# Routed stage of a fused two-layer kernel: the down product one slot later, both transpositions side by side, three homes for expert weights

## The reference

```python
def _moe_forward(hidden_states, gate_w, w_gate, w_up, w_down, sw_gate, sw_up, sw_down):
    x = hidden_states.reshape(-1, d)                  # 2048 x 512
    scores = jax.nn.softmax(x @ gate_w, axis=-1)
    topk_w, topk_idx = jax.lax.top_k(scores, K)       # K = 2 of E = 8
    comb = comb.at[jnp.arange(T)[:, None], topk_idx].add(topk_w)
    g = jax.nn.silu(jnp.einsum('td,edh->teh', x, w_gate)) * jnp.einsum('td,edh->teh', x, w_up)
    routed = jnp.einsum('teh,ehd,te->td', g, w_down, comb)   # h = 352
    shared = jax.nn.silu(x @ sw_gate) * (x @ sw_up) @ sw_down
    return (routed + shared).reshape(b, s, d)
```

## Time and profile before

| | us |
|---|---|
| median of the runs, and their range | 1068.06 (1067.4 to 1068.07) |
| the profiled execution | 1068.25 |
| its span, from the first to the last record | 1066.5 |
| TensorE busy in it | 1018.3 |
| first gather of tile 2 to the end of TensorE's work (routed stage) | some 782 to 1050 |
| last record of POOL, which issues the last scatter_add | 1057.7 |

### The profile page before, as it was taken

One profiled execution on the slowest core, in us unless ns is written; L12 is line 12 of the kernel. 1 busy time (PEld: TensorE's weight loads), 2 busy tenths in 40 slices (PEclk: granted clock), 3 DMA queues, 4 the chain that ended last, 5 costly groups with the idle time before them and its releaser, 6 DMA issues.

```text
span 1066.5 us, 14883 instructions
## 1 busy us (share of the span) xinstructions
PE 1018.3 (95%) x4893; PEld 842.1 (79%) x4895; DVE 527.5 (49%) x884; ACT 315.0 (30%) x550; POOL 360.8 (34%) x353
## 2 busy tenths in 40 slices
PE   8889999999999999999989999999989999999993
PEld 5668887888888887888757777778878999999992
DVE  3688877455575555545666333574551324442100
ACT  3733332111121112111232020301044454455551
POOL 4213344510000000000243000022067988988873
PEclk9989999999999999999999999999999999999997
DMA  6676643544333434454336000003255565665443
GB/s 210 211 244 207 201 130 116 170 133 144 132 126 113 156 131 162 130 178 138 117 110 194 30 12 32 9 0 114 106 164 151 158 158 108 143 152 148 79 59 40
DMA packets 51322, 136.41 MB, mean 128 GB/s; under 512 B 8708, under 2 KB 10004, under 8 KB 50772
## 3 DMA queue, kind: packets, MB, share of 16 engines
q1 hardware_dynamic: 37268, 109.22, 30.2%
q0 software_dynamic: 12432, 25.71, 12.2%
q10 hardware_dynamic: 1584, 1.02, 0.3%
HBM read 96.85 MB, written 39.07 MB: 127 GB/s over the span
## 4 chain that ended last, share of the span: by engine, by line
PE 81%; POOL 6%; DMA 4%; DVE 3%; issue 2%; ACT 1%; SPq 1%; PEldq 0%; POOLq 0%; PEld 0%; DVEq 0%; ACTq 0%
PE ps_y L1657 6%; PE ps_y L1659 6%; PE ps_y L1658 6%; PE ps_h L1617 5%; PE ps_h L1616 5%; PE ps_h L1615 5%; PE ps_u L1670 3%; PE ps_u L1669 3%; DMA out_x<-yt,slot_tok 2%; PE ps_y L1826 2%; POOL xg_lo L759 2%; PE ps_y L1827 2%; PE ps_h L1810 2%; PE ps_h L1903 2%; PE ps_h L1811 2%
## 5 line engine op out<-in xcount | busy, mean ns | idle before, releaser
L1192 DVE TENSOR_TENSOR h<-h,wb 128x512 f32<-128x512 f32 x64 | 44.4, 694 | 170.7 <-ACT h L898 163.7
L892 ACT ACTIVATE h<-ps_h,bias 128x512 f32<-128x512 f32 x64 | 44.0, 689 | 235.1 <-PE ps_h L1624 235.1
L1657 PE MATMUL ps_y<-w_hi,g_hi 128*128 (+1 forms) x256 | 103.2, 403 | 10.2 <-DVE g_lo L1200 10.2
L1659 PE MATMUL ps_y<-w_hi,g_lo 128*128 (+1 forms) x256 | 102.4, 400 | 0.0
L1658 PE MATMUL ps_y<-w_lo,g_hi 128*128 (+1 forms) x256 | 102.2, 399 | 0.0
L1615 PE MATMUL ps_h<-xt_hi,w_hl 128*128 128x512 f32 x256 | 100.0, 391 | 0.7 <-ACT lg_t L841 0.7
L1617 PE MATMUL ps_h<-xt_hi,w_hl 128*128 128x512 f32 x256 | 100.4, 392 | 0.0
L1616 PE MATMUL ps_h<-xt_lo,w_hl 128*128 128x512 f32 x256 | 100.2, 391 | 0.0
L1450 DVE CAST eg_hi<-e_raw 128x704 fp32r<-128x704 f32 x32 | 17.1, 594 | 136.9 <-PE ps_y L1928 124.5
L898 ACT ACTIVATE h<-ps_h,bias 128x512 f32<-128x512 f32 x64 | 43.9, 688 | 116.0 <-PE ps_h L1637 116.0
L753 POOL DMA_INDIRECT out_x<-yt,slot_tok x39 | 62.8, 1611 | 24.0 <-issue 12.0
(11 more groups left out here) (318 smaller groups left out, 2521.1 us busy)
## 6 DMA issues: line engine op xcount, KB each, us to landing
w_hl<-w1s_d SPq DMA_DIRECT2D x49, 704.0 KB, 4.1
w1s_d<-w_hl SPq DMA_DIRECT2D x16, 704.0 KB, 5.9
e_raw<-in_wgu SPq DMA_DIRECT2D x8, 1408.0 KB, 7.3
w_raw<-in_w1b SPq DMA_DIRECT2D x16, 608.0 KB, 4.7
x_in<-in_x SPq DMA_DIRECT2D x4, 1024.0 KB, 6.4
xres<-in_x SPq DMA_DIRECT2D x16, 256.0 KB, 4.5
acc<-x_d SPq DMA_DIRECT2D x4, 1024.0 KB, 8.0
xc_d<-xc SPq DMA_DIRECT2D x4, 1024.0 KB, 5.0
```

The source lines that it names most:

```text
L892: nc.scalar.activation(h0[u][:], ps_h[:, u, :], ACT.Gelu_apprx_tanh, bias=bias1[:, f:f + 1])\
L1192: tt(h1[u][:], h1[u][:], wb[:, v, :], ALU.mult).then_inc(gch, 1)
L1657: mm(ps_y[:, j, :], g_hi[u][:, cols], sl(w2_hi), start=first, **kw)
L1659: mm(ps_y[:, j, :], g_lo[u][:, cols], sl(w2_hi), start=False, **kw)
```

## The change

- In slot t TensorE now runs gate(t+1), up(t+1), turn_x(t+2), turn_g(t), down(t-1). The down product comes one slot after its transposition. In the last slots down(36), down(37), turn_g(38) and down(38) follow each other.
- `rgt_hi` and `rgt_lo` exist twice. ACT runs silu(t+1), up copy, x_high(t+2), g_high(t), weigh(t-1). POOL runs x_low(t+2), products(t+1), g_low(t), gather(t+5), scatter_add(t-1).
- Expert weights have three homes, 0, 2 and 3, of one tensor `expert`; the small buffers lie in the place of home 1. Expert e waits for the last tile of expert e-3.
- The home of an expert is e mod 3 and no longer e mod 2, which can't be read from the packed number by a bit. So `count_tokens` makes a second packed table, `home_tab` (base 4), after `etab`; TensorE's program waits for both and reads both. `WINDOW` is 6 instead of 5, since a pass of four slots now needs the experts of six tiles. Five slots are written out ahead of the loop instead of four.

```diff
-    WINDOW = 5
+    WINDOW = 6
+    HOMES = (0, 2, 3)
...
             for t in range(SLOT_TILES):
-                g_low(t)
+                if t + 2 < SLOT_TILES:
+                    x_low(t + 2)
                 if t + 1 < SLOT_TILES:
                     products(t + 1)
-                if t + 2 < SLOT_TILES:
-                    x_low(t + 2)
+                g_low(t)
...
                 if nxt:
                     silu(t + 1, 1 - u)
-                g_high(t, first=stored is None and n == 0)
-                if nxt:
                     up(t + 1, 1 - u)
                 if nxt2:
                     x_high(t + 2)
-                weigh(t, n, stored)
+                if nxt:
+                    g_high(t, u, first=isinstance(t, int) and t == 0)
+                if not isinstance(t, int) or t:
+                    weigh(t - 1, (n - 1) % 4, stored)
...
                 nc.vector.tensor_copy(etab[:], etab_g[:]).then_inc(etab_ok, 1)
+
+                dve.wait_ge(etab_ok, 1)
+                for turn in (6.0, 3.0):
+                    link(nc.vector.tensor_scalar(etab_g[:], etab_f[:], turn, -3.0, ALU.is_ge, ALU.mult))
+                    link(tt(etab_f[:], etab_f[:], etab_g[:], ALU.add))
+                link(nc.vector.tensor_scalar(etab_g[:], etab_f[:], 1.0, None, ALU.is_ge))
+                link(tt(etab_f[:], etab_f[:], etab_g[:], ALU.add))
+                link(nc.vector.memset(etab_g[:], 0.0))
+                link(nc.vector.tensor_copy(etab_g[:, 0:windows], etab_f[:, WINDOW - 1:ETAB]))
+                for n in reversed(range(WINDOW - 1)):
+                    link(nc.vector.scalar_tensor_tensor(out=etab_g[:, 0:windows], in0=etab_g[:, 0:windows],
+                                                        scalar=4.0, in1=etab_f[:, n:n + windows],
+                                                        op0=ALU.mult, op1=ALU.add))
+                nc.vector.tensor_copy(home_tab[:], etab_g[:]).then_inc(etab_ok, 1)
...
-                if e >= 2:
-                    tiles = dve.value_load(last_tile[0:1, e:e + 1], min_val=0, max_val=SLOT_TILES)
+                if e >= 3:
+                    tiles = dve.value_load(last_tile[0:1, e - 1:e], min_val=0, max_val=SLOT_TILES)
...
-            pe.wait_ge(etab_ok, 1)
+            pe.wait_ge(etab_ok, 2)
...
-                packed = pe.value_load(etab[0:1, bass.ds(t, 1)], min_val=0, max_val=E ** WINDOW - 1)
-                return [(packed // E ** n % E, packed // E ** n % 2) for n in range(WINDOW)]
+                names = pe.value_load(etab[0:1, bass.ds(t, 1)], min_val=0, max_val=E ** WINDOW - 1)
+                places = pe.value_load(home_tab[0:1, bass.ds(t, 1)], min_val=0, max_val=4 ** WINDOW - 1)
+                return [(names // E ** n % E, places // 4 ** n % 4) for n in range(WINDOW)]
...
-            def slot_tile(t, u, x_buf, n, this, after, nxt=True, nxt2=True):
...
-                if nxt:
-                    gate_or_up(t + 1, 1 - u, after, 0)
-                turn_g(t)
-                if nxt:
-                    gate_or_up(t + 1, 1 - u, after, 1)
+            def slot_tile(t, u, x_buf, n, behind, after, nxt2=True):
...
+                gate_or_up(t + 1, 1 - u, after, 0)
+                gate_or_up(t + 1, 1 - u, after, 1)
                 if nxt2:
                     turn_x(t + 2, x_buf, n)
-                down_routed(t, u, this)
+                turn_g(t)
+                if behind is not None:
+                    down_routed(t - 1, 1 - u, behind)
```

More of the change, by code:

```diff
@@ L1895, in gate_or_up, with w @@
                 o = (ps_h, ps_y)[k][:, u, 0:H1]
[L1896 removed]
+                def w(low, c):
+                    at = low * GU + (2 * c + k) * H1
+                    return expert[:, bass.ds(b, 1), at:at + H1].rearrange("p a n -> p (a n)")
                 for c in range(DC):
[L1898 to L1899 removed]
+                    mm(o, xg_hi[:, c, :], w(0, c), start=(c == 0), stop=False)
+                    mm(o, xg_hi[:, c, :], w(1, c), start=False, stop=False)
                 if k == 0:
@@ L1902, in gate_or_up @@
                 for c in range(DC):
-                    last = mm(o, xg_lo[:, c, :], w(eg_hi, c), start=False, stop=(c == DC - 1))
+                    last = mm(o, xg_lo[:, c, :], w(0, c), start=False, stop=(c == DC - 1))
                 last.then_inc((rgate_done, rup_done)[k], 1)
@@ L1950, in _ @@
             pe.wait_ge(sy_read, NS * TPS)
-            ahead = WINDOW - 1
-            for t in range(ahead):
-                slot_tile(t, t % 2, (t + 2) % 4, ((t + 2) // 4 + 1) * 16, e[t], e[t + 1])
-            with pe.Fori(1, (SLOT_TILES - 2) // ahead) as m:
-                e = experts(m * ahead)
-                for u in range(ahead):
-                    slot_tile(m * ahead + u, u % 2, (u + 2) % 4, (m + (u + 2) // 4 + 1) * 16, e[u], e[u + 1])
-            rest = range((SLOT_TILES - 2) // ahead * ahead, SLOT_TILES)
-            e = experts(SLOT_TILES - WINDOW)[WINDOW - len(rest):] + [None]
-            for n, t in enumerate(rest):
-                slot_tile(t, t % 2, (t + 2) % 4, ((t + 2) // 4 + 1) * 16, e[n], e[n + 1],
-                          t + 1 < SLOT_TILES, t + 2 < SLOT_TILES)
+            for t in range(5):
+                slot_tile(t, t % 2, (t + 2) % 4, ((t + 2) // 4 + 1) * 16, e[t - 1] if t else None, e[t + 1])
+            with pe.Fori(1, (SLOT_TILES - 3) // 4) as m:
+                e = experts(m * 4)
+                for n in range(4):
+                    slot_tile(m * 4 + 1 + n, (1 + n) % 2, (n + 3) % 4, (m + (n + 3) // 4 + 1) * 16, e[n], e[n + 2])
+            rest = range((SLOT_TILES - 3) // 4 * 4 + 1, SLOT_TILES)
+            first = SLOT_TILES - WINDOW
+            e = experts(first)
+            for t in rest[:-1]:
+                slot_tile(t, t % 2, (t + 2) % 4, ((t + 2) // 4 + 1) * 16, e[t - 1 - first], e[t + 1 - first],
+                          t + 2 < SLOT_TILES)
+            last = SLOT_TILES - 1
+            down_routed(last - 1, (last - 1) % 2, e[last - 1 - first])
+            turn_g(last)
+            down_routed(last, last % 2, e[last - first])
 _OUT = (32, 64, 512)
```

87 lines of the change are left out of this document (50 added, 37 removed).

## The result

The change makes the kernel slower. The median is 1084.95 us (1079.05 to 1087.74, four runs) against 1067.73 (1065.99 to 1068.07, four runs) of the kernel before in the same comparison: a ratio of 1.0174, 95% interval 1.0139 to 1.0208. I had forecast 1069.9 with a range to 1074.0. The sign of my sum was right and its size was not; the result lies 15 us above it and outside the range.

What follows compares the result with a forecast made beforehand. TensorE, busy 1018.3 of 1066.5 us, was taken to bound the kernel. The terms 3.5 + 1.9 - 2.5 - 0.5 - 0.3 - 0.3 = +1.8 us on the median of 1068.06 gave 1069.9 us, range 1065.4 to 1074.0.

Steps and rivals of the forecast that it cites:

- Steady slots: Routed stage on TensorE: a slot in which nothing waits stays at some 6.75 us, since regrouping transpositions saves nothing.
- Place 1: Second table in `count_tokens`, outside the routed stage: TensorE's wait grows from 2.1 to 5.2 us; costs 3.5 us with the clock.
- Place 2: Start of the routed stage: no down product covers the preparation of tile 2 any more; a loss of 1.9 us.
- Place 3: Slots 3 to 5: POOL held by the first scatter_add's landing stalls TensorE less than before; 2.5 us back, bounds 0 and 4.6.
- Place 4: Loop heads: `g_low`, made a slot ahead, lets TensorE's program run ahead and hides the head; 0.5 us back.
- Rival 2: Loop heads lie bare because TensorE's program cannot run far enough ahead: nine at 0.9 us, some 1078 us; chance 0.11.
- Place 5: Steady slots: `x_low` waits beside splits shrink slightly, earlier splits give TensorE nothing; 0.3 us back, bounds 2.3 back and 2 lost.
- The end: Last slots: slot 37 starts earlier, but the chain of the last scatter_adds' landings sets the end; 0.3 us back.
- rival 3: Faster: slack absorbs everything, no clock fall at the start, no `x_low` waits; 1065.8 us, 1064 with Place 1 lowest; chance 0.14.
- Rival 1: Slower: POOL stays behind, the first scatter_add is stuck as long and `x_low` stops TensorE; 2.5 us more, 1072.4 us; chance 0.22.

## Why the prediction was wrong, point by point

- **Steady slots** stay at 6.70 us: right. I took 6.75; that the 6.79 of every second slot goes too was not in the sum.
- **Place 1, the second table, +3.5:** right. `sh_g` moved by 3.3, the wait came in two pieces of 5.2 together, the clock fell to 0.50 over 712 to 716, and by the gate product of tile 1 TensorE was 3.7 us late.
- **Place 2, the start, +1.9:** right in kind, too small. It is 3.1, and places 1 and 2 together are 6.8 instead of 5.4. The gather is waited for 2.53 us instead of 1.70, and the clock is 0.58 over 794 to 797, a loss of 1.3, which I had not put a price on here.
- **Place 3, the first scatter_add, 2.5 back:** the mechanism was there as described, with `x_low(5)` behind a scatter_add that could start only 8.7 us after the one before (806.06 to 814.73), and a wait of 1.56 us, in a slot of 8.53. I had counted 1.5 for that slot; it was 1.8.
- **Place 4, the loop's head, 0.5 back:** right. No idle "issue" stands ahead of a gate product in the loop and nothing waits for `rgt_lo`. Rival 2, the bare heads, did not happen.
- **Place 5, POOL, ACT and the homes, 0.3 back, bounds 2.3 back and 2 lost: this is the step that failed.** I had treated the late landing of place 3 as an event of the start and taken from the trace of before that no later load holds POOL. That held only because five of its six loads fall into a gap between two scatter_adds, as the late-load run of the kernel before shows: with the load moved, POOL is held at all six there too. My text has the sentence that three homes move two splits forward and nothing else; it never asked where the load behind each split falls against the scatter_adds of the new order. They fell badly at six loads instead of one. The kernel before was lucky there, by 0.3 us of phase, and I had taken its luck for a rule. And "a delay is worked off just as slowly" left out who stands directly behind it: `x_low`, which gets through 1.1 to 1.3 us of a hold unnoticed where `g_low` got 1.8. On top comes the clock, which fell behind four of the six waits. Five further slots of 9.3 to 11.1 us cost 19.4 us above 6.70, against a lower bound of 2 lost.
- **The end, 0.3 back:** 0.6.

One sum of the rivals was off too: rival 3 with place 1 at its lower bound is 0.8 us below 1065.8, so 1065.0 and not 1064. It changes no chance.

Rival 1 named the right engine (POOL stays behind, for want of reserve) and priced it for one load, 2.5 us. Six times that on top of 1069.9 is 1084.9, the measured median; since the price of one load was that of place 3 undone and not that of a wait and its clock, such a hit would have been half luck. What is shown: that the loads are necessary (without them 1062.1), that pacing them removes the waits with the order left as it is, and that the old order passes some 0.7 us less of a hold on. What stays open is why a scatter_add that is issued from 1.1 us ahead of a load's start to 3.8 us behind it lands so late while one 1.4 ahead or 5 behind doesn't. The Trainium skill ("DMA: Bandwidth & Descriptors", section "Queues, rings and completion order") says that a DMA engine takes the queues it has work for in turn, a packet at a time. By that rule the depth of the load's own queue should hardly matter to a scatter_add on another. Here it does: with three of seven pieces under way in place of the whole load, at the same phase and the same 284 to 288 GB/s, POOL is held 1.31 us instead of 3.50. For this mix the measurement decides against the rule as I read it, unless the size of the transfers did it; with two pieces and with one the DMA engines also idle between them, so that the further fall, from 11.5 to 9.0 and 4.7 us, has two possible causes.

## What to carry to other kernels

When a change reorders an engine that issues DMAs, list each large transfer and ask where it falls against the small ones that are waited for, in the new order and not in the old; a load that does no harm today may only be lucky in its phase. Put the step with the least reserve as far as possible from the instruction that waits for a DMA. A transfer that isn't urgent can be handed out in pieces, a few under way at a time, and the number is to be measured: here, of seven pieces, two under way were worth 0.2% before the change and 1.5% after it, and one under way made the kernel slower.

## What the runs showed of the hardware

- A wait of TensorE of 2.3 us cost 4.1: the granted clock of the next 5 us is 0.69. Another of 2.35 us cost 2.6, with the clock at 1.00 behind it. In the kernel before with late loads, a wait of 1.10 us and a gap of 0.76 behind it made a slot of 10.64 us out of 6.70. The six waits of the changed kernel, 13.7 us together, cost 21.3.
- A scatter_add of 256 KB beside a load of 2.1 MB lands 7.9 to 9.2 us after its issue, at the six loads of the changed kernel; the median over all 39 is 4.9, and without any load it is 4.8 and the longest 5.7. With two pieces of the load under way the longest is 6.8.
- Pieces of 352 KB land in 3.1 us one at a time and in 4.0 with two under way.
- The slots of the new order are 6.70 us each; those of the old one alternate with 6.79 and 7.2. Without loads the sum above 6.70 falls from 8.9 to 1.6 us; my places 3 to 5 had 3.3 of that.
- `x_low` directly behind a scatter_add is listed with 1.84 to 1.89 us instead of 1.29 also where no split runs. It starts 1.05 us after the scatter_add, inside its span; from the start of the scatter_add to the end of `x_low` it is 2.9 us with either (844.40 to 847.29, and 905.60 to 908.53).
